# The last stage's moments on VectorE, the power alone on GpSimd, and every row tile stored by itself from SyncE

## The reference

```
out  = jnp.zeros_like(xf).at[rows, tok_dims].set(delta)   # 16 of 1024 channels per token
y    = x + out
# then, over the 1024 channels of each token:
m, v = mean(y), var(y)
y    = (y - m) / sqrt(v + 1e-5)
```

## Time and profile before

| what | us |
|---|---|
| median of three runs, no profiler | 1307.9 |
| the profiled execution, own time | 1311.31 |
| its span, first to last instruction | 1309.2 |
| the last stage begins (SyncE's first load of a unit) | 1138.53 |
| last of 64 scatters issued | 1301.39 |

### The profile page before, as it was taken

The page is one execution under the profiler, slowest core; times in us unless marked ns, Lnnn a source line. Parts: engine busy times, 40 slices in busy tenths (PEclk is TensorE's granted clock), DMA queues, the critical chain, the costliest instruction groups (busy, mean ns, idle before and its releaser), DMA issues. The chain is left out here.

```text
span 1309.2 us, 31773 instructions
## 1 busy us (share of the span) xinstructions
PE 1158.9 (89%) x9346; PEld 735.1 (56%) x9346; DVE 1061.5 (81%) x2508; ACT 951.7 (73%) x1809; POOL 833.4 (64%) x1692
## 2 busy tenths in 40 slices
PE   5799999999999999999999999999999965588700
PEld 4556666666666666666666666666666632333100
DVE  4888889999999999999999999998988765586710
ACT  5657888888888888888888888888888743444760
POOL 3125666767676767676767676767676665335576
PEclk9989999999999999999999999999999977655555
DMA  4112222222222222222222222222222116689993
GB/s 141 34 37 102 103 103 104 102 102 102 102 102 102 102 103 106 106 106 106 106 106 106 106 106 106 106 106 106 106 105 102 71 65 234 230 316 352 419 409 125
DMA packets 64115, 175.05 MB, mean 134 GB/s; under 512 B 11580, under 2 KB 23108, under 8 KB 64071
## 3 DMA queue, kind: packets, MB, share of 16 engines
q1 hardware_dynamic: 49430, 138.85, 28.7%
q10 hardware_dynamic: 8496, 33.56, 6.6%
q0 software_dynamic: 6144, 2.11, 1.2%
HBM read 69.06 MB, written 101.20 MB: 130 GB/s over the span
## 5 line engine op out<-in xcount | busy, mean ns | idle before, releaser
L1052 DVE SCALAR_TENSOR_TENSOR acc<-xT_all,cw_sb,acc 128x256 f32<-128x256 f32 x768 | 354.3, 520 | 7.2 <-ACT acc L751 7.1
L777 ACT ACTIVATE sg<-TX,bet,gam 128x256 f16<-128x256 f32 x256 | 129.5, 556 | 42.2 <-PE TX L464 42.2
L484 PE MATMUL PR<-xT_all,w_sb 128*128 128x256 f32 x512 | 139.1, 396 | 2.9 <-ACT xT_all L715 2.9
L1384 POOL TENSOR_TENSOR AT<-AT,Wm 128x128 f32<-128x128 f32 x224 | 114.8, 512 | 41.7 <-DVE AT L1078 25.9
L496 PE MATMUL WK<-w_sb,tS 128*128 128x512 f32 x256 | 138.3, 622 | 0.0
L751 ACT ACTIVATE acc<-xT_all,cb_sb,cw_sb 128x256 f32<-128x256 f32 x256 | 132.5, 592 | 4.8 <-DVE xT_all L1038 2.8
L538 PE MATMUL OB<-th_all,AT 128*128 128x512 f32 x256 | 124.4, 609 | 11.7 <-POOL AT L1384 10.2
L566 PE MATMUL PR<-shT,w_mg_sb 128*64 128x128 f32 x2048 | 128.0, 278 | 6.5 <-ACT shT L760 6.5
L566 PE MATMUL PR<-shT,w_rk_sb 128*64 128x128 f32 x2048 | 125.9, 276 | 0.0
L566 PEld LDWEIGHTS PR<-shT,w_rk_sb 128*64 128x64 f32 x2048 | 110.5, 137 | 26.3 <-issue 26.3
L566 PEld LDWEIGHTS PR<-shT,w_mg_sb 128*64 128x64 f32 x2048 | 112.5, 138 | 18.9 <-issue 12.0
(11 more groups left out here) (230 smaller groups left out, 2665.1 us busy)
## 6 DMA issues: line engine op xcount, KB each, us to landing
xin_all<-in_x SPq DMA_DIRECT2D x32, 1024.0 KB
y_ring<-y_all SPq DMA_DIRECT2D x32, 1024.0 KB, 4.1
y_scratch<-y_all SPq DMA_DIRECT2D x32, 1024.0 KB, 6.1
own<-y_scratch SPq DMA_DIRECT2D x5, 2048.0 KB, 16.1
out<-own ACTq DMA_DIRECT2D x5, 2048.0 KB, 19.9
rows<-y_scratch SPq DMA_DIRECT2D x4, 2048.0 KB, 12.3
out<-rows ACTq DMA_DIRECT2D x4, 2048.0 KB, 13.6
RX<-RE SPq DMA_DIRECT2D x128, 32.2 KB
```

The costliest lines, as they stand in the source:

```text
L484: i = pe.matmul(PR[:, 0:T], w0_sb[:, blk, :], xT[b][:, blk, HIST:HIST + T], start=(blk == 0), stop=(blk == NB - 1))
L777: nc.scalar.activation(sg[:, blk, :], TX[:, (blk % 2) * T:(blk % 2 + 1) * T], ACT.Sign, scale=gam[:, blk:blk + 1], bias=bet[:, blk:blk + 1 ...
L1052: v.scalar_tensor_tensor(acc[:, blk, :], xT[b][:, blk, i:i + T], cw_sb[:, blk, i:i + 1], acc[:, blk, :], ALU.mult, ALU.add).then_inc(e_con ...
L1384: q.tensor_tensor(late, late, Wm[:, :, l, :].rearrange("p c (n h) -> p c n h", h=h), ALU.add)\
```

## The change

Three things are changed, all in the last stage. First, VectorE computes the moments: `moments(k)` are five small instructions behind the sums of a batch, then GpSimd does the power alone (`deviation`, one instruction), and VectorE computes `coef0`, `coef1` and `o_off` from it in `coefficients(k)`. These, and `corrections(k)`, stand in the next batch behind the first pass of `chosen`'s loop (`between`), for the last batch at its end. Second, `BEHIND` becomes (0, 1, 3, 6, 9, 9, U): units 4 and 5 are scattered behind the power of batch 3, units 6 to 8 behind that of batch 4, none behind that of batch 5. Third, SyncE issues all the stores, one for each row tile as soon as it is scaled (`p_row`), and the loads of units 8 to 14 come between the stores: the load of unit `u + 6` stands behind the four stores of unit `u`, and waits until unit `u - 2` is stored.

```diff
+            def loaded(u):
+                return 16 * (u // NS + 1)
             def stored(u):
-                return 16 * (u // NS + 1)
+                return 4 * loaded(u)
...
-                for u in range(NS, U - 1):
-                    sp.wait_ge(p_st[slot_id(u)], stored(u - NS))
-                    load(u)
+                for u in range(U - 1):
+                    for n in range(4):
+                        sp.wait_ge(p_row, 4 * u + n + 1)
+                        sp.dma_start(out_u[u, :, n, :], slot(u)[:, n, :]).then_inc(p_st[slot_id(u)], 16)
+                    old = u - 2
+                    if 0 <= old and old + NS < U - 1:
+                        sp.wait_ge(p_st[slot_id(old)], stored(old))
+                        load(old + NS)
+                for n in range(4):
+                    sp.wait_ge(p_row, NC - 4 + n + 1)
+                    sp.dma_start(out_u[U - 1, :, n, :], last_slot[:, n, :]).then_inc(p_sl[n], 16)
...
-                def moments(k):
+                def deviation(k):
                     at = slice(starts[k], starts[k + 1])
                     pool.wait_ge(p_sum, k + 1)
-                    q.tensor_scalar(mean_n[:, at], sums[:, 0, at], -1.0 / D, 0.0, ALU.mult, ALU.add)
...
+                    q.tensor_tensor(rs[:, at], var[:, at], mh[:, at], ALU.pow).then_inc(p_m, 1)
...
-                BEHIND = (0, 1, 3, 4, 6, 9, U)
+                BEHIND = (0, 1, 3, 6, 9, 9, U)
...
-                        if u == U - 1:
-                            act.wait_ge(p_row, n + 1)
-                            nc.scalar.dma_start(out_u[u, :, n % 4, :], row).then_inc(p_sl[n % 4], 16)
-                        elif n % 4 == 3:
-                            act.wait_ge(p_row, n + 1)
-                            nc.scalar.dma_start(out_u[u], slot(u)).then_inc(p_st[slot_id(u)], 16)
...
+                        if s0 == lo // 2 and between is not None:
+                            coefficients(between)
+                            corrections(between)
+                def moments(k):
+                    at = slice(starts[k], starts[k + 1])
+                    if k == 0:
+                        dve.wait_ge(p_i, 2)
+                    link(v.tensor_scalar(mean_n[:, at], sums[:, 0, at], -1.0 / D, None, ALU.mult))
+                    v.scalar_tensor_tensor(var[:, at], sums[:, 1, at], 1.0 / D, ss4[:, at], ALU.mult, ALU.add)
+                    v.tensor_tensor(c_off[:, at], nr[:, at], mean_n[:, at], ALU.add)
+                    link(v.tensor_tensor(m_sq[:, at], mean_n[:, at], mean_n[:, at], ALU.mult))
+                    v.tensor_tensor(var[:, at], var[:, at], m_sq[:, at], ALU.subtract).then_inc(p_sum, 1)
+                def coefficients(k):
+                    at = slice(starts[k], starts[k + 1])
+                    dve.wait_ge(p_m, k + 1)
+                    v.tensor_tensor(coef0[:, at], r2[:, at], rs[:, at], ALU.mult)
+                    v.tensor_tensor(coef1[:, at], c_off[:, at], rs[:, at], ALU.mult).then_inc(p_coef, 1)
+                    link(v.tensor_tensor(o_off[:, at], mean_n[:, at], rs[:, at], ALU.mult))
```

More of the change, by code:

```diff
@@ L1632, in _ @@
                 pool.wait_ge(p_gi, 1)
-                BEHIND = (0, 1, 3, 4, 6, 9, U)
+                BEHIND = (0, 1, 3, 6, 9, 9, U)
                 for k in range(len(BATCHES)):
-                    moments(k)
+                    deviation(k)
                     for u in range(BEHIND[k - 1] if k else 0, BEHIND[k]):
@@ L1697, in _ @@
                         if n % 4 == 0 and u != U - 1:
-                            act.wait_ge(r_ld[slot_id(u)], stored(u))
+                            act.wait_ge(r_ld[slot_id(u)], loaded(u))
                         row = slot(u)[:, n % 4, :]
@@ L1761, in cells, with chosen @@
                     link(b)
-                def chosen(lo, hi, k):
+                def chosen(lo, hi, k, between):
                     ready = [0, 0]
@@ L1804, in per_token, with batch @@
                         return a[:, at].unsqueeze(2).to_broadcast([P, n, DS])
-                    dve.wait_ge(p_coef, k + 1)
                     link(v.tensor_tensor(outs[:, at, :], w_o[:, at, :], per_token(rs), ALU.mult))
                     v.tensor_tensor(outs[:, at, :], outs[:, at, :], per_token(o_off), ALU.add).then_inc(p_out, 1)
-                def batch(k):
+                def batch(k, between):
                     lo, hi = starts[k], starts[k + 1]
                     n = hi - lo
-                    chosen(lo, hi, k)
+                    chosen(lo, hi, k, between)
                     dve.wait_ge(p_zf, hi // 2)
@@ L1822, in batch @@
                     v.scalar_tensor_tensor(w_o[:, lo:hi, :], x, 2.0, d, ALU.mult, ALU.add)
-                    v.tensor_reduce(sums[:, 1, lo:hi], w, AX_X, ALU.add).then_inc(p_sum, 1)
+                    link(v.tensor_reduce(sums[:, 1, lo:hi], w, AX_X, ALU.add))
+                    moments(k)
                 ready = 0
@@ L1831, in _ @@
                         ready = min(ready + 1, len(RANGES) - 1)
-                    batch(k)
-                    if k:
-                        corrections(k - 1)
+                    batch(k, k - 1 if k else None)
+                coefficients(len(BATCHES) - 1)
                 corrections(len(BATCHES) - 1)
```

## The result

The changed kernel has a median of 1318.4 us over seven runs (1315.16 to 1320.14), the one before 1308.1 (1306.86 to 1313.64). The ratio is 1.0056, 95% interval 1.0041 to 1.0072: slower by 7.3 us, 5.4 to 9.4. The two medians alone lie 10.3 us apart; the text goes by the ratio, to which the traces are nearer. The forecast was +2.6. The profiled execution has an own time of 1318.52 and a span of 1316.8, against 1311.31 and 1309.2: +7.2 and +7.6.

The account below looks back on a forecast made before the run. GpSimd's last 28 scatters were taken as the bound, stores close behind. Unit 8 landing at 1256.7 plus 13.1 us starts them at 1269.8, the last at 1304.0 against 1301.39: +2.6 us, median 1310.5, range 1305 to 1315.

Parts of the forecast that it names:

- What bounds before: End of the last stage: GpSimd's 28 scatters (34.2 us) set the end, last row store landing 12 us ahead.
- Moments to VectorE: VectorE's batches: no cost taken up to batch 3, but later coefficients; unit 3 starts at 1194.75, first row done at 1196.0.
- The hold: GpSimd waits at unit 8's scatters, delaying both powers and the 28 scatters; 13.1 us from landing to the 28.
- Eleven transfers until unit 8 has landed: SyncE's queue: stores 3 to 8 and loads 9 to 13, full from 1196.0, have landed at 1256.7.
- a sign of being wrong: Unit 8's landings 5 us off, shown by windows over 428 or under 370 GB/s, would make the prediction wrong.
- "The stores of units 9 to 15 don't hold them": Last 28 scatters: the last store lands at 1301.0, ahead of its scatter at 1304.0, so stores don't delay them.
- The 5.6 us for a unit in row stores: SyncE's queue: time assumed per unit of row stores, from unit 15's four landings 1.4 us apart.
- Rival 1: Row stores cost more than unit 15's did, 6.26 us a unit: stores decide, +8.7 us, 1316.6; chance 0.13.
- Range: Median time of the changed kernel, forecast to lie between 1305 and 1315 us.
- the two bounds: End of the kernel: last scatter behind the hold at 1304.0, last store landing at 1301.0.
- The about 2.0 us: Fixed part of each DMA, beside 1.2 us of data; 12.8 us a unit if nothing overlapped, which unit 15's landings opposed.

Follow-up runs that it names:

- e3: The kernel before with only the moments moved to VectorE, stores, loads and scatter order as before; ratio to before 0.9981.
- e14: The changed kernel with loads of units 8 to 14 issued from ScalarE's queue, each once unit u's fourth row is scaled; ratio to before 1.0042.
- e7: The changed kernel with one 2048 KB store per unit in SyncE's queue instead of four of 512 KB, unit 15 still by rows; ratio to before 1.0063.
- e9: The changed kernel with the load of unit u + 6, still waiting for unit u - 2's stores, ahead of unit u's stores; ratio to before 1.0050.
- e13: The changed kernel with the load of unit u + 6 ahead of unit u's stores and the scatters in their old places; ratio to before 1.0031.
- e12: The kernel before without the 28 scatters of units 9 to 15, so its output lacks them; 1287.46 us in one run.
- e5: The changed kernel with the load of unit u + 7, waiting for unit u - 1's stores, ahead of unit u's stores; ratio to before 1.0155.

## Why the prediction was wrong

- **What bounds before:** right. GpSimd's 28 scatters end it, the stores lie 12 us below. (The stage has 26 transfers of a unit, 10 loads and 16 stores, not 27, and 60 of the small stores are new, not 64; no sum uses either number.)
- **Moments to VectorE:** right. ScalarE starts unit 3 at 1194.73 (1194.75 foretold), unit 3's first row store is issued at 1195.99 (1196.0). That it fits to hundredths is luck: the stage of after began 0.7 us sooner than that of before. e3, this part alone, gains 2.5 us.
- **The hold:** the mechanism stands as foretold, from the 6.9 us ahead of unit 8's scatters to VectorE's 18.7. From the landing (1260.4) to the first of the 28 it took 12.4 us, 13.1 foretold.
- **Eleven transfers until unit 8 has landed:** the step that failed, in size. I had 60.7 us from 1196.0, the landing latency in it; it took 64.4 (1196.0 to 1260.4). Of the 3.7 us, 2.7 lie in the first three transfers, which took 19.0 us instead of 16.3 (unit 4's rows have landed by 1216.6, 0.7 us ahead of its first scatter), in the windows with 303 and 328 GB/s; 1.0 lies in the other eight. Unit 8 landed less than the 5 us off that I had set as a sign of being wrong; the windows under 370 GB/s that went with that sign did show. Why these were slow stays open (below).
- **"The stores of units 9 to 15 don't hold them":** failed as well. The last row was to have landed at 1301.0, SyncE sees it at 1304.7. The same lateness carried on: the 28 scatters were stopped for 2.0 us more than their 34.2. 3.7 + 2.0 - 0.7 are the 5.0 us by which the last scatter (1308.96) lies behind the 1304.0 foretold.
- **The 5.6 us for a unit in row stores** was taken from four stores of before beside which scatters ran, and it was applied to a queue in which loads and stores take turns. It was too little for the first three transfers and more than enough later: the windows from 1255 to 1280 have 413 to 417 GB/s, which is 5.1 us a unit. What made the start slow isn't the single queue: e14 has two and moves no more in the first 70 us (263 GB/s). And it isn't the size: e7 is no faster with 2048 KB.
- **Rival 1** gave +8.7, near the 7.3 measured, and unit 8 landed at 1260.7 (1260.4 measured). It took its rate from a window of before with 335 GB/s, and such windows did come back. But its cause, small stores that cost more than large ones, doesn't carry it: in e7 they are large and the time is the same.
- **Range:** 1305 to 1315. The median is 1318.4; by the ratio it would be 1315.2, just outside too. I had computed the two bounds 3 us apart and not added up that one slow start makes both late, the hold by 3.7 us and the scatters behind it by 2.0.

On rival 1, the Trainium skill, "DMA: Bandwidth & Descriptors", section "Rules for kernel authors", asks for 1 MiB or more per DMA; e7 with 2 MiB against 0.5 gains 14 GB/s in the full stretch and no time. The same section says that spreading DMAs over issuing engines doesn't help bandwidth; the full stretch of e14, 417 GB/s against 394 to 408 with one queue, points the other way by 2 to 6%, and in kernel time no gain clear of noise came of it. The about 2.0 us that the prediction takes from this page's section "Anatomy of one DMA" are given there for DMAs that GpSimd issues; these stores are SyncE's, and unit 15's four landings, 1.3 us apart in after (1300.7 to 1304.7), show no such part between stores that stand back to back.

What remains open is what slows the queue near 60 to 70 us of the changed kernel's stage. Before has such a window too (335), 41 us into its stage, and neither was traced to a cause. It isn't the scatters: from 1205 to 1210 after has 328 GB/s at a full DMA share, and GpSimd's queue moved nothing in that window. It goes with the order of the transfers: e9, where only the loads' places differ, has 408 and 400 GB/s from 1195 to 1205 in its own one queue, and its poor windows, 327 and 338, from 1180 to 1190. Nor is it shown why two queues move more than one in the full stretch.

## What to carry to other kernels

Before a load and a store path are joined in one in-order queue, add up from the trace how much each transfer must still carry when the queue first fills: what an empty stretch didn't move wasn't caught up here once the DMA engines were full. An early start on work that waits for late data (here scatters placed ahead of a short step that another engine needs) belongs behind that step. And when an edit that clearly removes a wait brings nothing, look for a second chain that ends at the same place, and undo both: here 0 and 1 us singly, 3.3 together, by ratios whose intervals (after's and e13's) overlap by 0.0005.

## What the runs showed of the hardware that I had not expected

- 64-byte scatters beside stores can cost the stores up to a tenth of their rate. The windows at the end of before have 397 and 368 GB/s with the scatters running; without the last 28 (e12) the same windows have 413 and 415, though the scatters themselves move only 7 GB/s. The loss sets in late: in after the 28 begin at 1272.80, and the window from 1275 still has 414 GB/s, that from 1285 has 368.
- An issuing engine's wait for its own youngest transfer is worse than it looks: e5's rounds of 13.9 us for the 4.2 MB of one load and four row stores, and 294 GB/s against 400 in e9, whose only difference is that the awaited stores are one unit older and the load one unit nearer.
- 512 KB stores cost the kernel no time against 2048 KB ones: 394 GB/s against 408 where the queue was full, 264 against 249 where it waited for rows (e7).
